# One-hot matrices of the picked columns: from VectorE's compares to ScalarE's relu(1 - |node - source|)

## The reference, cut to what matters

```
p1 = pool_max(relu(h @ Wp1.T + bp1));  x = relu(concat(h, p1) @ Wm1.T + bm1)
p2 = pool_max(x);  x = layernorm(relu(concat(x, p2) @ Wm2.T + bm2) + x)
p3 = pool_max(x);  x = layernorm(relu(concat(x, p3) @ Wm3.T + bm3) + x)
pool_max(h): for each node the maximum of h[src] over its edges (0 where it has none)
```

## Time and profile before

| what | value |
|---|---|
| median of 3 runs | 5100.06 us (5085.27 to 5100.75) |
| profiled execution: its time | 5097.23 us |
| profiled execution: its span | 5095.4 us |
| busy: PE, DVE, ACT, POOL | 2919.7, 3072.5, 1027.0, 3244.5 us |
| TensorE clock granted, mean | 0.82 |

### The profile page before, as it was taken

One profiled execution on the slowest core, in us unless ns is written; L12 is line 12 of the kernel. 1 busy time (PEld: TensorE's weight loads), 2 busy tenths in 40 slices (PEclk: granted clock), 3 DMA queues, 4 the chain that ended last, 5 costly groups with the idle time before them and its releaser, 6 DMA issues.

```text
span 5095.4 us, 62340 instructions
## 1 busy us (share of the span) xinstructions
PE 2919.7 (57%) x15472; PEld 2110.1 (41%) x15472; DVE 3072.5 (60%) x9028; ACT 1027.0 (20%) x2805; POOL 3244.5 (64%) x3289
## 2 busy tenths in 40 slices
PE   3120388767888777778777787777910006971100
PEld 2020276646766555556555565555710003431000
DVE  6754256657666778887788877888634332124433
ACT  1000100001000333335333343333510003420000
POOL 4767677776777377772777737776057773027776
PEclk6565699988999889999999999999965557985555
DMA  5656566665666433332333323333156662236665
GB/s 182 196 169 221 183 200 210 206 192 178 212 208 212 140 98 106 106 106 76 100 104 106 106 75 98 105 106 91 57 195 206 206 206 95 99 137 206 206 206 188
DMA packets 279687, 776.82 MB, mean 152 GB/s; under 512 B 64561, under 2 KB 103474, under 8 KB 275506
## 3 DMA queue, kind: packets, MB, share of 16 engines
q0 software_dynamic: 157104, 429.21, 30.1%
q1 hardware_dynamic: 122242, 343.62, 17.6%
HBM read 455.64 MB, written 316.93 MB: 152 GB/s over the span
## 4 chain that ended last, share of the span: by engine, by line
PE 29%; POOL 11%; DVE 10%; issue 7%; DMA 5%; ACT 1%; DVEq 1%; POOLq 0%; ACTq 0%; SPq 0%
POOL HC L497 10%; PE PS L1270 9%; PE PS L1262 7%; DVE W L1887 4%; PE PS L1196 3%; PE PS L959 3%; DMA HC<-table_typ,run_typ 3%; PE PS L1251 3%; DMA HC<-table_rel,run_rel 2%; DVE HC L1951 2%; DVE work L1895 1%; DVE score L1895 1%; PE PS L953 1%; PE PS L1158 1%; PE PS L1339 1%
## 5 line engine op out<-in xcount | busy, mean ns | idle before, releaser
L1708 DVE SCALAR_TENSOR_TENSOR HC<-HC,run_rst 128x256 f32<-128x256 f32 x1890 | 915.3, 484 | 1155.1 <-DMA HC<-table,run_max 496.2
L497 POOL DMA_INDIRECT HC<-table,run_max x1113 | 1144.1, 1028 | 442.4 <-issue 310.4
L473 POOL DMA_INDIRECT HC<-table,idx_src x648 | 636.6, 982 | 428.1 <-DMA table<-B 206.2
L1066 PE MATMUL PS<-AM,ring 128*128 128x256 f32 x3000 | 707.5, 391 | 147.2 <-DVE ring L1691 146.7
L473 POOL DMA_INDIRECT X<-table,idx_src x600 | 578.3, 964 | 183.5 <-issue 133.1
L1066 PEld LDWEIGHTS PS<-AM,ring 128*128 128x128 f32 x3000 | 568.1, 194 | 282.4 <-DVE ring L1691 206.7
L1951 DVE SCALAR_TENSOR_TENSOR HC<-HC,fcol,PS 128x257 f32 x1248 | 592.7, 475 | 152.7 <-PE PS L1270 134.6
L497 POOL DMA_INDIRECT HC<-table_typ,run_typ x391 | 378.8, 969 | 400.7 <-DMA table_typ<-HC 281.9
L1262 PE MATMUL PS<-AM,work 128*128 x3744 | 632.7, 281 | 0.0
L1100 PE MATMUL PS<-ident,HC 128*128 128x128 f32 x10 | 3.4, 445 | 1000.1 <-DVE HC L1708 1000.1
L497 POOL DMA_INDIRECT HC<-table_rel,run_rel x391 | 379.0, 969 | 298.8 <-DMA table_rel<-AM 179.8
(11 more groups left out here) (259 smaller groups left out, 4451.6 us busy)
## 6 DMA issues: line engine op xcount, KB each, us to landing
prefix<-HC SPq DMA_DIRECT2D x485, 512.0 KB, 3.2
table_typ<-HC SPq DMA_DIRECT2D x19, 1024.0 KB, 3.8
HC<-table,run_max POOLq DMA_INDIRECT x1113, 3.2
HC<-table,idx_src POOLq DMA_INDIRECT x648, 2.8
table<-AM SPq DMA_DIRECT2D x15, 640.0 KB, 3.5
table<-B SPq DMA_DIRECT2D x15, 640.0 KB, 3.3
X<-table,idx_src POOLq DMA_INDIRECT x600, 2.8
table_rel<-AM SPq DMA_DIRECT2D x10, 640.0 KB, 4.4
```

The lines of the kernel that those rows point to most:

```text
L473: pool.indirect_dma_start(held(t)[:, 0:D], None, table, bass.IndirectOffsetOnAxis(ap=idx_src[:, t:t + 1], axis=0)).then_inc(landed[t % AHE ...
L497: pool.indirect_dma_start(run_slot(k), None, src, bass.IndirectOffsetOnAxis(ap=run_idx[s[1]][:, j:j + 1], axis=0)).then_inc(landed[k], 16)
L1066: last = nc.tensor.matmul(PS[:, (2, 5)[c % 2], 0:D], quads[:, (QUADS * x + g) % 4, b % 4, :], A[:, b, :], start=(b == 0), stop=(b == BLOCK ...
L1708: V.scalar_tensor_tensor(run_slot(k), run_slot((j - 1) % SLOTS), run_rst[:, j:j + 1], fresh, fade, join).then_inc(pooled, 1)
```

## The change

The compares on VectorE go. For every block ScalarE computes the distance |node - source| with an Abs (128x128, `scale=-1`, the node numbers as bias), and for every quad one Relu over the four blocks, relu(1 - distance), which is 1 where they are equal and 0 elsewhere (the distances are whole numbers). The distances go to two halves of a new buffer `apart` in `work`. `far_src` has three places where it had four, and one use of `work` moves to another column. The function `picks_first` gives ScalarE the same rule that TensorE had for where the picks stand between blocks; TensorE's order stays what it was. ScalarE does the quads of a pick in front of the copy of the block at which the pick stands.

```diff
+        apart = work[:, 1024:2048].rearrange("p (h k e) -> p h k e", h=2, k=4)
-        far_src = sb("far_src", [P, 4, P], I32)
+        far_src = sb("far_src", [P, 3, P], I32)
@@ the order of picks, for both engines
+        def picks_first(s, i):
+            return sum(1 for j in picked_in(s) if 4 * (s[2] - 1) * (i - 1) + 3 > j - 12)
@@ SP
-                            if far >= 4:
-                                sp.wait_ge(quad_made, QUADS * (picks_before(n) + far - 3))
+                            if far >= 3:
+                                sp.wait_ge(quad_made, QUADS * (picks_before(n) + far - 2))
@@ ScalarE
+                    def distances(x):
+                        c, g = x // QUADS, x % QUADS
+                        act.wait_ge(far_in[c % 3], 16 * (far_before(n, c % 3) + c // 3 + 1))
+                        z = QUADS * picks_before(n) + x
+                        if z >= 2:
+                            act.wait_ge(quad_made, z - 1)
+                        for b in range(4 * g, min(4 * g + 4, BLOCKS)):
+                            last = nc.scalar.activation(apart[:, z % 2, b % 4, :], far_src[:, c % 3, :], ACT.Abs, bias=node_id[:, b:b + 1], scale=-1.0)
+                        last.then_inc(apart_made, 1)
+                    def make_quad(x):
+                        z = QUADS * picks_before(n) + x
+                        size = min(4, BLOCKS - 4 * (x % QUADS))
+                        if z >= 4 and (z - 4) % QUADS == QUADS - 1:
+                            act.wait_ge(picked, (z - 4) // QUADS + 1)
+                        elif z >= 4:
+                            act.wait_ge(quad_used, (z - 4) // QUADS * (QUADS - 1) + (z - 4) % QUADS + 1)
+                        act.wait_ge(apart_made, z + 1)
+                        nc.scalar.activation(quads[:, z % 4, 0:size, :], apart[:, z % 2, 0:size, :], ACT.Relu, bias=ones[:, 0:1],
+                                             scale=-1.0).then_inc(quad_made, 1)
+                    def make_quads(first, last):
+                        for x in range(QUADS * first, QUADS * last):
+                            if x == QUADS * first:
+                                distances(x)
+                            if x + 1 < QUADS * last:
+                                distances(x + 1)
+                            make_quad(x)
                     if s[2] > 1:
-                        for b in range(BLOCKS):
-                            act.wait_ge(turned2, u0 + b + 1)
-                            nc.scalar.activation(B_cols[:, :, cols(b)], halves(PS[:, 6 + b % 2, 0:D]), ACT.Copy).then_inc(spread2, 1)
+                        for i in range(BLOCKS + 1):
+                            make_quads(picks_first(s, i - 1) if i else 0, picks_first(s, i))
+                            if i < BLOCKS:
+                                act.wait_ge(turned2, u0 + i + 1)
+                                nc.scalar.activation(B_cols[:, :, cols(i)], halves(PS[:, 6 + i % 2, 0:D]), ACT.Copy).then_inc(spread2, 1)
+                        make_quads(picks_first(s, BLOCKS), len(picked_in(s)))
@@ VectorE
-                                V.tensor_tensor(quads[:, z % 4, 0:size, :], src, at, ALU.is_equal).then_inc(quad_made, 1)
-                        if j >= 13 and j % 12 in (0, 1, 3, 5, 7, 9, 11):
-                            next(quads_inside, None)
-                                split_row(1, TRS * D)
+                                split_row(1, 8 * D)
```

More of the change, by code:

```diff
@@ L335, in gnn_kernel @@
         fix_made = sem("fix_made")
-        far_in = [sem(f"far_in{k}") for k in range(4)]
+        far_in = [sem(f"far_in{k}") for k in range(3)]
+        apart_made = sem("apart_made")
         quad_made = sem("quad_made")
@@ L399, in far_before @@
         def far_before(n, k):
-            return sum(len(picked_in(s)[k::4]) for s in PLAN[:n])
+            return sum(len(picked_in(s)[k::3]) for s in PLAN[:n])
         def landings(n, k):
@@ L574, in _ @@
                         while far < len(picked_in(s)) and picked_in(s)[far] // 4 - 10 <= g:
-                            if far >= 4:
-                                sp.wait_ge(quad_made, QUADS * (picks_before(n) + far - 3))
-                            sp.dma_start(far_src[:, far % 4, :], picks[far:far + 1, :].to_broadcast([P, P])).then_inc(far_in[far % 4], 16)
+                            if far >= 3:
+                                sp.wait_ge(quad_made, QUADS * (picks_before(n) + far - 2))
+                            sp.dma_start(far_src[:, far % 3, :], picks[far:far + 1, :].to_broadcast([P, P])).then_inc(far_in[far % 3], 16)
                             far += 1
@@ L1068, in pick_rows @@
                                 last.then_inc(picked if g == QUADS - 1 else quad_used, 1)
-                        pick_now = 0
                         for i in range(BLOCKS + 1):
-                            while pick_now < len(picked_in(s)) and 4 * (s[2] - 1) * (i - 1) + 3 > PICKED[pick_now] - 12:
-                                pick_rows(pick_now)
-                                pick_now += 1
+                            for c in range(picks_first(s, i - 1) if i else 0, picks_first(s, i)):
+                                pick_rows(c)
                             if s[2] > 1 and i < BLOCKS:
@@ L1086, in _ @@
                                       [wide_w[:, c, :] for c in range(K2)]).then_inc(mm_done, 1)
-                        for c in range(pick_now, len(picked_in(s))):
+                        for c in range(picks_first(s, BLOCKS), len(picked_in(s))):
                             pick_rows(c)
@@ L1674, in inside @@
                                 yield
[L1676 to L1690, removed]
-                                V.tensor_tensor(quads[:, z % 4, 0:size, :], src, at, ALU.is_equal).then_inc(quad_made, 1)
-                                yield
-                    work_inside, quads_inside = inside(), make_quads()
+                    work_inside = inside()
                     for j in range(TILES):
```

## The result

The changed kernel takes 5072.7 us (median of 6), the kernel before 5096.5 (median of 6): ratio 0.9954, 95% interval 0.9937 to 0.9970 (one disturbed execution of the changed kernel, 5445 us, is in its median and not in the ratio). The profiled execution took 5075.44 us, 21.8 less than that of before, where 36.2 less was forecast. So it is faster, by half a per cent and by six tenths of what was forecast.

What follows compares the result with a forecast made beforehand. The prediction took POOL's gathers, issued end to end and stretched by VectorE's compares, to bound the kernel. From 5097.2 us it took 44.4 for shorter gathers and added 8 for the early picks: 5061 us, range 5042 to 5098.

Steps and rivals of the forecast that it cites:

- POOL waiting for the running maxima: Sign in max 2 and 3: POOL waiting over 0.3 us at a time for line 1708 means rival B or C.
- rival B: Part of the gain is eaten: ScalarE's pick costs 14.0 to 15.1 us, time 5088 us; chance 0.12.
- C: ScalarE becomes the slower bound through Relu, wait and four Abs: 16.9 us a pick, about 5200 us; chance 0.12.
- ScalarE's pick: ScalarE's Abs and Relu for one pick: 12.7 us (10.8 to 15.1), under the 14.0 us of twelve columns.
- the early picks: Picks between blocks in max 2 and 3 lose 17 and 20 us, just covered; +8 us charged in all.
- POOL issues gathers end to end, and compares stretch them: Line 497 in max 2 and 3: gathers fall from 1034 and 1027 to 969 ns, -44.4 us.
- Compare time in itself is worth nothing: VectorE's 210 compares a stage, 131.8 us: direct worth 0, as VectorE waits for landings.
- the cover of 20 us: POOL waits only when VectorE is 19 columns behind, 24 us, of which 4 are its usual distance.
- the edge: Crossing the cover of 20 us in max 2 and 3: 3 us a stage charged.
- Far_src with three places: SP's load waits for quads three picks back; POOL's slot reuse covers it: 0, up to 5 us.

Runs made afterwards that it cites:

- the pair of unused compares: Changed kernel plus 210 unused VectorE compares a stage, both inputs in SBUF or one in PSUM: ratios 1.0152 (repeated 1.0163) and 1.0268 to the kernel before.
- distances ahead: Changed kernel with ScalarE's distances always two quads ahead, across blocks too: 5045.3 us against 5089.1 (ratio 0.9909); 1.0234 in a long series.
- long series: Kernels run together on one chip, the unchanged kernel before beside them taking 5936, 5946, 5983 and 5939 us.
- sources in PSUM: Kernel before, compares still on VectorE, but reading source numbers first copied to PSUM: ratios 1.0096, 1.0088, 1.0080 and 1.0087 to the kernel before.
- short series: Kernels run together on one chip, the unchanged kernel before beside them taking 5089 and 5100 us.

## Why the prediction was right, and where its size was off

It gave 5061 us, range 5042 to 5098; 5072.7 came, the sign and the mechanism as argued. The range was wide enough to take in a term three times its forecast, so it says nothing for that term. One of its signs pointed wrong: POOL waiting for the running maxima was to mean rival B or C, but ScalarE's pick kept its 12.7 us and the waits came from the early picks.

- *POOL issues gathers end to end, and compares stretch them.* Right: 44.8 us measured against 44.4. Shown by the pair of unused compares. The Trainium skill ("SBUF — State Buffer", "Who interferes with whom") holds in its rule on two SBUF inputs against a GpSimd read; its inference that a tensor_tensor doesn't delay descriptor generation doesn't hold for these gathers: 1052 against 965 ns.
- *Compare time in itself is worth nothing.* Right, as the sum above closes without such a term: VectorE lost the 131.8 us of compares in max 2, and its wait for landings rose from 177.6 to 193.6 us there.
- *ScalarE's pick.* 12.7 us forecast, 12.68 measured; table loads are 17 in the whole program, as before, none from Abs.
- *The early picks: +8 us.* This is the term that was mis-sized; it measured +23. Place, direction and chain were right (copies, then ScalarE's start, TensorE, line 1691, running maxima, POOL). The period was short by 1.0 us in max 2 (16.9 for 17.9) and by 1.6 a pick in max 3 (30.7 for 34.0 a pair). In max 2 two slips explain it: I let TensorE finish 2.2 us after the sixth quad is ready, as if it were idle then, but it is still in the fifth; from ScalarE's start to TensorE's end are 3.2 + 12.0 = 15.2 us, not 14.3. And ScalarE starts 2.7, not 2.6, us after the pick's end. In max 3 the lower clock adds 0.7 us at seven of fifteen picks, which the forecast didn't have; the stage's mean of 0.92 (0.93 before) hides it. With six losses of 3.9 us, 23 us, and fifteen of 3.0, 45 us, the cover of 20 us is overrun; I had 17 and 20, both just inside, and charged 3 us for the edge. Two figures just under a limit should have been priced as likely over it. The run with distances ahead shows this term: 2.3 us less a pick in max 2, 3.1 in max 3, and the waits are gone.
- *Far_src with three places: 0.* Right, but only as a consequence of the above: SP waited 22 and 26 us, and the wait fell to 1.3 and 2.0 when the early picks were quicker; four places by themselves ran only in a long series.

## What to carry to other kernels

If GpSimd issues gathers without a pause, look at the duration of the gather in stages with different company on VectorE, not at VectorE's busy time: an instruction there with two SBUF inputs costs the gather what it still has to run when the gather starts (less about 0.13 us here), and moving one input to PSUM, or the work to ScalarE, takes that away. When work moves to an engine with an ordered queue, reckon it twice: its steady pace, and how late it can start where its queue is tied to another engine, as that, and not the pace, ate half of this gain. A pipeline's preparation that needs nothing from the other engine belongs in front of the wait for it; here that was one loop's order, and some 23 us. And a gain of half a per cent holds for the condition in which it was measured: in the long series the relatives of the changed kernel were slower than the kernel before, by 2.3% with distances ahead and by 2.8% with four places of far_src; the changed kernel itself never ran there.

## What was not expected of the hardware

In four series of six the kernel before took 0.84 to 0.89 ms longer, and the one with distances ahead, which met both kinds, 1.03 ms. This is where POOL stood in one of them (sources in PSUM, max 2):

```profile
960.95 0.95 POOL L497 DMA_INDIRECT HC<-table,run_max  x1 [0.30 <-issue]
969.59 1.11 POOL L497 DMA_INDIRECT HC<-table,run_max  x1 [7.69 <-DMA prefix<-HC]
```

There the order of the kernels is another: the kernel before is the fastest of those run, and the long gathers beat the short ones by 63 us (6029 against 6092). It would fit that gathers issued faster put other transfers further back where these are the limit, but the traces speak against slow transfers. In stage rel, where all kernels have the same code, the last packet of a gather ends 1.4 to 2.6 us after its instruction in the traces of either kind (all but one in a hundred gathers at each end); the same line 1708 (1728 and others in the changed kernels), there the sum of its column, starts 1.7 to 3.6 us after it in the short series, and 20 to 24 us after it from the middle of the stage on in the long ones. So the data is there, and VectorE goes on late. TensorE's clock isn't it in that stage either, since TensorE does nothing there and 0.50 is granted in both; over the whole program the mean is 0.76 in the long series and 0.82 in the short. What delays the engines stays open.
